# Cross-attention and expert block on one core: context and rows laid out turned by the host, LayerNorm finished on turned rows

## The reference, cut to what matters

```
x: (32, 112, 256)    ctx: (32, 375, 192)          # all float32
h   = layernorm(x)                                # over 256, no gain or bias
q   = (h @ Wq),  k = ctx @ Wk,  v = ctx @ Wv      # 8 heads of 64, inner 512
p   = softmax(q k^T / 8)                          # 112 x 375 for a head
x   = x + (p v) @ Wout + bout
h   = layernorm(x)
out = x + sum over 2 of 8 experts of w_e * ((h @ W1_e) * silu(h @ W3_e)) @ W2_e
        + ((h @ Ws1) * silu(h @ Ws3)) @ Ws2       # shared expert
```

## Time and profile before

| | |
|---|---|
| median of three runs | 1144.96 us |
| profiled execution, first to last instruction | 1154.2 us |
| mean granted clock of TensorE | 0.986 of full speed |
| attention (to about) | 690 us |
| one pass of `body` in steady state | 40.1 us |
| HBM read and written | 74.40 MB, 49.68 MB |

### The profile page before, as it was taken

The page is one execution under the profiler, slowest core; times in us unless marked ns, Lnnn a source line. Parts: engine busy times, 40 slices in busy tenths (PEclk is TensorE's granted clock), DMA queues, the critical chain, the costliest instruction groups (busy, mean ns, idle before and its releaser), DMA issues. The chain is left out here.

```text
span 1154.2 us, 26175 instructions
## 1 busy us (share of the span) xinstructions
PE 1097.8 (95%) x7534; PEld 967.9 (84%) x7534; DVE 766.7 (66%) x2024; ACT 691.0 (60%) x1667; POOL 694.4 (60%) x629
## 2 busy tenths in 40 slices
PE   5989999999999999999999889999999999999996
PEld 4778888888888888888888779999888888888886
DVE  4778888888888888888888756675633333333332
ACT  4777777777777777777777754542233443443332
POOL 3797778768777877787787745665223333333333
PEclk9999999999999999999999998989999999999999
DMA  5223143133214322331342339222465336333861
GB/s 150 82 59 97 57 132 103 56 106 120 89 57 131 109 71 85 125 99 49 123 139 70 118 119 339 92 73 87 134 200 136 55 56 162 57 58 58 258 173 15
DMA packets 103698, 124.04 MB, mean 107 GB/s; under 512 B 19712, under 2 KB 71888, under 8 KB 103632
## 3 DMA queue, kind: packets, MB, share of 16 engines
q1 hardware_dynamic: 83376, 99.82, 26.6%
q0 software_dynamic: 11760, 15.15, 7.4%
q10 hardware_dynamic: 8496, 8.22, 2.5%
HBM read 74.40 MB, written 49.68 MB: 108 GB/s over the span
## 5 line engine op out<-in xcount | busy, mean ns | idle before, releaser
L520 POOL TENSOR_TENSOR probs<-probs,inv_sum 112x750 f32<-112x750 f32 x128 | 183.8, 1437 | 134.5 <-DVE inv_sum L974 134.4
L1726 POOL DMA_INDIRECT out<-stage,to_row x48 | 74.9, 1559 | 173.5 <-ACT stage L1778 125.2
L2006 DVE TENSOR_TENSOR hT_lo<-banks,hT_hi 128x512 fp32r<-128x512 f32 x63 | 43.6, 691 | 184.5 <-ACT hT_hi L1770 178.6
L690 ACT ACTIVATE probs<-banks,neg_max 112x375 f32<-112x375 f32 x256 | 145.9, 573 | 18.3 <-DVE neg_max L961 15.4
L961 DVE TENSOR_REDUCE neg_max<-banks 112x2 f32<-112x750 f32 x128 | 119.8, 936 | 47.7 <-PE banks L1320 46.0
L487 POOL TENSOR_TENSOR v_both<-v_raw,v_both 125x512 fp32r<-125x512 f32 x96 | 123.2, 1284 | 7.5
L1346 PE MATMUL banks<-ident,probs 112*125 112x112 f32 x768 | 106.9, 275 | 12.7 <-DVE pT L967 12.7
L1334 PE MATMUL banks<-pT,v_both 125*128 125x224 f32 x768 | 114.0, 284 | 5.1 <-DVE oT_lo L992 5.0
L1334 PEld LDWEIGHTS banks<-pT,v_both 125*128 125x128 f32 x768 | 99.2, 192 | 23.2 <-issue 21.4
L967 DVE TENSOR_TENSOR pT<-banks,pT 125x672 fp32r<-125x672 f32 x128 | 108.6, 849 | 14.4 <-ACT pT L681 13.1
L1346 PEld LDWEIGHTS banks<-ident,probs 112*125 112x125 f32 x768 | 97.0, 189 | 24.1 <-issue 20.0
(11 more groups left out here) (292 smaller groups left out, 3206.0 us busy)
## 6 DMA issues: line engine op xcount, KB each, us to landing
w_split_scratch<-stage SPq DMA_DIRECT2D x16, 1536.0 KB, 8.2
ring<-w_split_scratch SPq DMA_DIRECT2D x16, 1536.0 KB
stage<-in_L_ffn_W SPq DMA_DIRECT2D x48, 256.0 KB, 2.9
ctx_in<-in_ctx SPq DMA_DIRECT2D x32, 281.2 KB
xg<-x_sorted_scratch ACTq DMA_DIRECT2D x59, 136.0 KB
x_in<-in_x SPq DMA_DIRECT2D x16, 224.0 KB, 2.5
x_res<-in_x SPq DMA_DIRECT2D x32, 112.0 KB, 2.1
x_scratch<-x SPq DMA_DIRECT2D x32, 112.0 KB, 1.9
```

What stands on the lines that cost most here:

```text
L520: pool.tensor_tensor(probs[:, two, :], probs[:, two, :], inv_sum[:, 2 * s:2 * s + 2].rearrange("p (e o) -> p e o", o=1).to_broadcast([N, 2 ...
L690: act.activation(probs[:, h % 4, :], S_BANKS[0:N, e, 0:M], ACT.Exp, bias=neg_max[:, h:h + 1], accum_out=row_sum[:, h:h + 1]).then_inc(exp_ ...
```

## The change

The host now lays out the inputs: context comes as `ctxT` (for each batch 128 partitions, two blocks of 376 columns: channels 0 to 127, and channels 128 to 191 twice, with a zero last column), rows come both as `x` and turned as `xT`, and the weights come in the layout of their buffers, so that each needs one DMA instead of two or three. The turning units are gone from all lists. In their place:

- ACT `ctx_hi` copies `ctx_in` to `cT_hi` (128x752, SBUF to SBUF), DVE `ctx_lo` subtracts (128x752, both inputs in SBUF), twice in a pass.
- The mean and 1/deviation of each row lie along partitions, but turned rows need them along columns. So SP stores `mean_var` to DRAM (`store_stats`, 112x4), waits for it, and loads it back spread over 128 partitions (`load_stats`, 128x448, into `stat_all`). POOL `centre` subtracts the mean from `xT_in`, DVE `scale_rows` multiplies, ACT `xT_high` and DVE `xT_low` split.
- `xT_in` and `stat_all` lie in `x1_second`, whose own load (second chunk of the experts' rows) now comes after the last pass.

The products are as many and as large as before. `experts` is not touched.

```diff
-PROLOGUE = ["c00", "c10", "k00", "k10", "k20", "k30", "v00", "xt0", "xt1", "v10", "q0", "c01", "c11"]
+PROLOGUE = ["k00", "k10", "k20", "k30", "v00", "v10", "q0"]
...
+            def store_stats(p):
+                sp.dma_start(stat_dram[bass.ds(p, 1), :, :, :].rearrange("o n b j -> n (o b) j"), mean_var[:]).then_inc(stat_stored, 16)
+            def load_stats(p):
+                sp.dma_start(stat_all, stat_dram[bass.ds(p, 1), :, :, :].rearrange("o n b j -> o (n b j)").to_broadcast(
+                    [128, 2 * N2])).then_inc(stat_loaded, 16)
...
+                sp.wait_ge(rstd_ready, p + 2)
+                store_stats(p + 1)
                 if two_more:
-                    sp.wait_ge(xn_ready, p + 2)
                     sp.dma_start(x_in[:], x_rows(2 * p + 4, 2)).then_inc(x_loaded, 16)
+                sp.wait_ge(stat_stored, 16 * (p + 2))
+                sp.wait_ge(scaled, p + 1)
+                load_stats(p + 1)
...
                 if two_more:
-                    sp.wait_ge(unit_made, unit_count(p, False, "c11"))
+                    sp.wait_ge(ctx_ready[1], p + 2)
                     load_ctx(2 * p + 5, 1)
...
+            def centre(n):
+                pool.wait_ge(stat_loaded, 16 * n)
+                pool.wait_ge(xT_loaded, 16 * n)
+                pool.tensor_tensor(xT_halves, xT_halves, for_columns(0), ALU.subtract).then_inc(centred, 1)
...
                 normalise(p, 2)
+                centre(p + 2)
                 run(p, False, "v11")
...
+            def ctx_hi(i, n, p=None):
+                act.wait_ge(ctx_loaded[i], 16 * n)
+                if p is not None:
+                    act.wait_ge(unit_made, unit_count(p, False, ("v20", "k31")[i]))
+                act.activation(cT_hi[i][:], ctx_in[i][:], ACT.Copy).then_inc(ctx_hi_ready[i], 1)
...
+            def scale_rows(n):
+                dve.wait_ge(centred, n)
+                dve.tensor_tensor(xT_halves, xT_halves, for_columns(1), ALU.mult).then_inc(scaled, 1)
+            def ctx_lo(i, n):
+                dve.wait_ge(ctx_hi_ready[i], n)
+                dve.tensor_tensor(cT_lo[i][:], ctx_in[i][:], cT_hi[i][:].bitcast(F32), ALU.subtract).then_inc(ctx_ready[i], 1)
...
-                run(p, False, "c00")
+                ctx_lo(0, p + 2)
                 maximum(p, 2)
...
-                run(p, False, "c01")
-                run(p, False, "c11")
+                ctx_lo(1, p + 2)
                 low_of_sums(p, 5)
```

More of the change, by code:

```diff
@@ L37 @@
 UNIT_BANKS = 3
-PROLOGUE = ["c00", "c10", "k00", "k10", "k20", "k30", "v00", "xt0", "xt1", "v10", "q0", "c01", "c11"]
-UNITS = ["v20", "k01", "k21", "q1", "k11", "c00", "v01", "v11", "w1", "xt0", "c10", "v21", "k31", "xt1", "k20",
-         "k00", "k10", "k30", "v00", "q0", "w0", "v10", "c01", "c11"]
+PROLOGUE = ["k00", "k10", "k20", "k30", "v00", "v10", "q0"]
+UNITS = ["v20", "k01", "k21", "q1", "k11", "v01", "v11", "w1", "v21", "k31", "k20", "k00", "k10", "k30", "v00", "q0",
+         "w0", "v10"]
 LAST_UNITS = ["q1", "v20", "k31", "k01", "k11", "v21", "v11", "v01", "k21", "t0", "t1", "w1", "g0", "g1", "u1",
@@ L149, in build @@
     xs_dram = nc.dram_tensor("x_sorted_scratch", (E * CAP, ROW), F32, kind="Internal").ap()
+    stat_dram = nc.dram_tensor("stat_scratch", (PAIRS, N, 2, 2), F32, kind="Internal").ap()
     top = ExitStack()
@@ L301, in split_lo @@
             eng.wait_ge(aw_hi, n + 1)
-            rows = slice(0, 64) if kind in "kv" and i == 1 else slice(0, 128)
-            lo, hi, w = piece(W_LO[kind], kind, i)[rows], piece(W_HI[kind], kind, i)[rows].bitcast(F32), staged(n, kind)[rows]
+            lo, hi, w = piece(W_LO[kind], kind, i), piece(W_HI[kind], kind, i), staged(n, kind)
+            if kind in "kv" and i == 1:
+                lo, hi, w = hi[64:128], hi[64:128], w[64:128]
+            hi = hi.bitcast(F32)
             if kind == "q":
@@ L320, in batch_in @@
         def batch_in(name):
-            return int(name[2]) if name[0] in "ckv" else None
+            return int(name[2]) if name[0] in "kv" else None
         def heads_of(name):
@@ L350, in load_ctx @@
             def load_ctx(b, i):
[L351 to L361, removed]
+                sp.dma_start(ctx_in[i][:], ctx_of(b)).then_inc(ctx_loaded[i], 16)
@@ L375, in _ @@
             sp.dma_start(x_res[1][:], x[1]).then_inc(res_loaded[1], 16)
-            sp.wait_ge(xn_ready, 1)
-            sp.dma_start(x_in[:], x_rows(2, 2)).then_inc(x_loaded, 16)
-            sp.wait_ge(unit_made, PROLOGUE.index("c10") + 1)
+            sp.wait_ge(ctx_ready[0], 1)
             load_ctx(2, 0)
-            sp.wait_ge(unit_made, PROLOGUE.index("c11") + 1)
+            sp.wait_ge(xT_ready, 1)
+            load_xT(1)
+            sp.wait_ge(ctx_ready[1], 1)
             load_ctx(3, 1)
@@ L503, in _ @@
             rstd_of(1)
-            for n in (2, 3):
-                split_lo(pool, n)
+            split_lo(pool, 2)
+            centre(1)
             for n, name in enumerate(PROLOGUE):
@@ L849, in statistics @@
             def statistics(n):
+                wait(dve, stat_stored, 16 * (n - 1))
                 dve.wait_ge(x_loaded, 16 * n)
@@ L1062, in body @@
                 add_most(p, 1)
-                run(p, False, "c10")
+                scale_rows(p + 2)
                 reciprocal(p, 4)
@@ L1070, in body @@
                 add_most(p, 2)
-                run(p, False, "xt1")
+                xT_low(p + 2)
                 run(p, False, "k20")
```

277 lines of the change are left out of this document (142 added, 135 removed).

## The result

| | before | after |
|---|---|---|
| median, same chip | 1144.91 us | 1211.63 us (1208.87 to 1213.52, 4 runs) |
| ratio of the two | | 1.0567, interval 1.054 to 1.0594 |
| span of the profiled execution | 1154.2 us | 1208.9 us |
| mean granted clock | 0.986 | 0.944 |
| one pass in steady state | 40.05 us | 44.38 us |

A forecast was written before the change was run, and what follows sets the result against it. PE was taken to bound the kernel, nearly without holes. A pass: - 1.91 + 0.95 + 1.01 + 0 = + 0.05; 15 passes + 0.8, prologue - 2.0, together - 1.2 from 1144.96: 1143.8 us, range 1121 to 1160.

The forecast's parts named there:

- The shedding: On PE, 16 transposes and the slow first products behind them go: 1.91 us less in a pass.
- cost A: At ctx_lo(0), DVE waits for POOL's normalise(1), so PE stands 0.95 us longer at turn_probs(1) in each pass.
- first rival: DVE's tensor-tensor subtractions do not wait for POOL; 1.1 us gained in a pass, 1126.5 us in all; chance 0.27.
- wait from nothing to a whole POOL instruction: Bounds on DVE's wait beside POOL, read from normed in the first pass; the full wait was taken.
- the clock is granted in full in the slices: Reason for giving only 3% to the change freeing nothing because clock or loads bind, and all else.
- holes of 1.6 and 1 us: PE's hole at turn_probs(1) grown from 0.63 to about 1.6 us, and a new one at turn_probs(7), costing 1.01.
- Cost B: At ctx_lo(1), DVE waits for POOL's split_piece, so PE stands 1.01 us at turn_probs(7) in each pass.
- The trip: Statistics stored to DRAM and loaded back for POOL's centre; POOL waits 0.5 us, hidden by 0.1 us, costed at nothing.
- each us: Each us the statistics land beyond 364.9 costs PE a us at turn_probs(3) in each pass.
- second rival: Statistics return late from DRAM, POOL waits at centre; 0.9 us in each of 15 passes, 1157 us; chance 0.23.
- Prologue: Before the passes: earlier keys nearly cancelled by q0's wait for statistics; 4 us less to 3 more, 2 less taken.
- Sum: A pass + 0.05 us, 15 passes + 0.8, prologue - 2.0, together - 1.2 us.

The follow-up runs named there:

- e1: Changed kernel with the even batch's subtraction ctx_lo(0) cut to 8 columns in the passes, both operands kept; ratio 1.0252 to the kernel before.
- e6: Changed kernel with ctx_lo(0) in the passes replaced by a reduction over the same 752 columns, one SBUF input; ratio 1.0316 to the kernel before.
- e7: Changed kernel with ctx_lo(0) moved behind low_of_probs(2), ctx_hi(1) and ctx_lo(1) behind k00, nothing left out; ratio 1.0188 to the kernel before.
- e2: Changed kernel with ctx_lo(0) moved from ahead of maximum(2) to behind low_of_probs(0), nothing left out; ratio 1.0325 to the kernel before.
- e5: Changed kernel without the store and load of the statistics in the passes; ratio 1.0511 to the kernel before.
- e13: Kernel before with three idle DVE reductions from PSUM (0.85 us each) ahead of maximum(2) in every pass; ratio 1.0488 to the kernel before.

## Why the prediction was wrong

**The shedding** (-1.91 a pass) was right in kind: the third stretch of the table is shorter although k01 waits 0.71 in it. - 0.70 - 0.71 = - 1.41, so 0.50 of the 1.91 did not show; small waits are the likely place, not added up one by one.

**The wait between DVE and POOL, cost A**, is the first step that failed. Mechanism and place were right, and the first rival (no wait) fell with e1 and e6. The size was not: "wait from nothing to a whole POOL instruction" took one instruction for the upper end, from a row in which POOL had a single instruction to finish. At 392.85 the next one stood right behind, and DVE lost to that too. The hole grew by 1.98, not 0.95: the difference is 1.03, and the second instruction takes 1.04. That it would stand there could be read before the run, from the timeline of POOL in the kernel before, directly behind the `normalise` of 357.64:

```profile
359.04 1.04 POOL L483 TENSOR_TENSOR v_both<-v_raw,one 125x512 fp32r<-125x512 f32 x1
```

**The clock** is the second, a term that the sum lacked, and the larger part: 3.01 us a pass. The prediction read "the clock is granted in full in the slices" as a reason against a clock problem. It was the state of passes whose holes are 0.63 us. Having forecast holes of 1.6 and 1 us, it should have asked what follows a hole. The trace of the kernel before had a case, in its last stretch (timeline of PE, then a window of it; the clock records have the fall from 651.9 on):

```profile
650.26 0.43 PE L1320 MATMUL banks<-k_hi,q_hi 64*112 64x376 f32 x2 [1.82 <-ACT probs L690]
```

```profile
652.00:655.00 3.00, 3.00 (x16) 3.00 (x15) 2.43 (x8) 2.22 (x7) 2.92 (x3) 0.50 0.70 210
```

It also had a hole of 2.45 us in the first pass (before 69.28) with no fall behind it, so that trace showed the risk and not the price. With A at 0.95, a hole of 1.6, some falls were likely: of e7's five holes of 1.4 to 1.7 us at `turn_probs(3)` two have one behind them. How many is not shown.

**Cost B** (1.01 at `turn_probs(7)`) came as 0.71 at k01. `ctx_lo(1)` took 1.32 us, held by `split_piece` as forecast, but the first that waits for it on PE is k01, which the text didn't ask. 0.3 less than forecast.

**The trip** (costed 0) costs 0 in the kernel after, but by the longer hole, not by its own merit. With the hole away POOL waits 1.3 (e2) to 2.3 us (e6) in a pass, not 0.5, and PE stands 1.7 and 1.5 at `turn_probs(3)`: the place is the forecast one, "each us" for "a us of PE" holds only roughly. The landing is 3.3 us where 2.5 were taken, that of `x_in` ahead of it 3.5 instead of 2.5. The second rival was thus right in kind for a kernel in which A is small. `centre` takes 1.39 us, not 1.2; the Trainium skill's half as much again for a step of 16 bytes (GPSIMD Engine Reference, "Performance pitfalls for Q7 kernels") would have been about 1.8, an estimate from the 1.2. The trace agrees with neither.

**Prologue** (-2): the first product came 6.3 us earlier, at 7.62 instead of 13.95, but PE stood 7.27 us for q0's `xT_lo`, and the first scores started at 27.78 instead of 26.88. It lost 0.9, part of it to the clock, which stands at half from 18.5 to 28.7 us, in and behind that wait. At `turn_probs(1)` of the last pass the kernel after is 62.3 us behind (663.79 against 601.48), at the end 54.7; where the 7.6 come back this study did not look into.

**Sum as measured**, a pass: - 1.91 + 1.98 + 3.01 + 0.71 + 0.50 = + 4.29, by 15 about + 64; 54.7 in the spans. The range ended at 1160 because each hole was priced only by its own length.

## What to carry over

A us of hole on TensorE may cost more than a us: before you accept a new wait of 1 to 3 us, look at what the granted clock does behind holes of that length, or put one there by idle work and measure. When two engines hold each other off, as DVE and POOL do here, ask how many of the neighbour's instructions stand in a row, not how long one is. And when a hole goes, look what was hidden in it: here the trip through DRAM, then a late maximum; the gain, 0.7% of the time, came only when all three were placed.

## What the runs showed of the hardware that was not expected

- An 8-column subtraction with two SBUF inputs, 0.17 us when nothing holds it, takes until POOL's current and next instruction have ended (1.98 us); a 752-column reduction with one SBUF input at the same place takes 0.94.
- DVE does not always lose to a POOL instruction that follows at once. In the kernel after, `ctx_lo(0)` lost the change from L544 to L507 but won the next, from L507 to L511, 1.04 us later; `ctx_lo(1)` won the first change it met, and the POOL instruction then took 1.43 us (0.74 alone):

```profile
382.00 1.32 DVE L912 TENSOR_TENSOR cT_lo<-ctx_in,cT_hi 128x752 fp32r<-128x752 f32 x1 [0.36 <-ACT cT_hi L649]
```

```profile
381.23 1.29 POOL L524 TENSOR_TENSOR stage<-stage 128x512 fp32r<-128x512 f32 x1
382.48 1.43 POOL L517 TENSOR_TENSOR x_res<-x_res,bout_sb 112x256 f32<-112x256 f32 x1
```

  What decides this was not found.
- TensorE's clock falls to half behind one hole in a queue that is otherwise nearly full: in no pass for 0.9 us, in 5 of 13 for 2.0, in 10 of 12 for 2.94, and in every one from the third on for the 2.61 of the kernel after. The same hole can have a fall of 3.4 us, of 6.8 us or none behind it, by where in time it lies (e5, e13).
